# Attention in float32r: two pieces instead of three bfloat16 ones, two heads in the halves of the array's rows, rotation and split on GpSimd

## What is computed

```
qkv = (x @ Wqkv).reshape(b, l, 3, H, DH)          # H = 16 heads, DH = 16
q, k, v = (qkv[:, :, 0], qkv[:, :, 1], qkv[:, :, 2])
q = q * cos + rotate_half(q) * sin
k = k * cos + rotate_half(k) * sin
scores = jnp.einsum('bqhd,bkhd->bhqk', q, k) * DH ** -0.5
attn = jax.nn.softmax(scores, axis=-1)
out = jnp.einsum('bhqk,bkhd->bqhd', attn, v).reshape(b, l, d) @ Wo
x = _layernorm(x + out)
...                                                # RMS norm, shared block, top-2 of 8 experts
x = _layernorm(x + ffn(x))
```

## Time and profile before

| | us |
|---|---|
| median of 3 runs | 1294.05 (1291.84 to 1295.58) |
| span of the profiled execution, first to last instruction | 1291.3 |
| start to first exponential | 53.1 |
| attention, first exponential to the last transposes of its output | 53.1 to 569 |
| everything behind attention | some 722 |

### The profile page before, as it was taken

One profiled execution on the slowest core, in us unless ns is written; L12 is line 12 of the kernel. 1 busy time (PEld: TensorE's weight loads), 2 busy tenths in 40 slices (PEclk: granted clock), 3 DMA queues, 4 the chain that ended last, 5 costly groups with the idle time before them and its releaser, 6 DMA issues. The chain is left out here.

```text
span 1291.3 us, 29542 instructions
## 1 busy us (share of the span) xinstructions
PE 1224.3 (95%) x9440; PEld 934.5 (72%) x9440; DVE 976.6 (76%) x1925; ACT 996.4 (77%) x2043; POOL 583.9 (45%) x590
## 2 busy tenths in 40 slices
PE   4899999999999999979899969999999999999997
PEld 3444444444444444337899969999999999999897
DVE  6888887888788888728676648777777777777596
ACT  6699998999899999846654437777777777777687
POOL 6332322232223220005467745666666666666763
PEclk8899999999999999988899979999999999999999
DMA  9300000010000000433022246777777777776363
GB/s 298 117 19 19 18 19 20 2 35 3 19 2 19 2 18 3 144 104 117 18 91 100 87 158 197 260 251 253 246 238 238 235 249 253 253 239 217 101 218 119
DMA packets 125414, 161.28 MB, mean 125 GB/s; under 512 B 17088, under 2 KB 108224, under 8 KB 125312
## 3 DMA queue, kind: packets, MB, share of 16 engines
q1 hardware_dynamic: 118496, 141.25, 33.7%
q0 software_dynamic: 6816, 18.75, 4.1%
HBM read 122.06 MB, written 37.52 MB: 124 GB/s over the span
## 5 line engine op out<-in xcount | busy, mean ns | idle before, releaser
L546 DVE TENSOR_REDUCE att_mx<-att_psA 128x1 f32<-128x512 f32 x512 | 337.8, 683 | 75.5 <-PE att_psA L331 74.9
L461 ACT ACTIVATE att_prob<-att_psB 128x512 f32<-128x512 f32 x512 | 299.7, 600 | 54.0 <-PE att_psB L341 41.0
L341 PE MATMUL att_psB<-att_qk 128*128 128x512 bf16 x512 | 197.6, 388 | 12.8 <-issue 5.6
L1648 ACT ACTIVATE exp_psU<-exp_psU,ew_b 128x256 f32<-128x256 f32 x312 | 126.6, 447 | 103.7 <-PE exp_psU L1605 103.7
L331 PE MATMUL att_psA<-att_qk 96*128 96x512 bf16 x512 | 196.9, 386 | 3.0 <-DVE att_mx L546 3.0
L1699 DVE CAST exp_hh<-exp_psU 128x512 fp32r<-128x512 f32 x156 | 107.9, 692 | 101.9 <-ACT exp_psU L1648 101.9
L1588 PE MATMUL exp_psD<-exp_w2h,exp_hh 128*128 128x256 f32 x624 | 175.8, 282 | 0.0
L1603 PE MATMUL exp_psU<-exp_xh,exp_w1h 128*128 128x256 f32 x624 | 173.7, 278 | 1.4 <-DVE exp_xl L1690 1.4
L1605 PE MATMUL exp_psU<-exp_xh,exp_w1l 128*128 128x256 f32 x624 | 173.4, 278 | 0.0
L1604 PE MATMUL exp_psU<-exp_xl,exp_w1h 128*128 128x256 f32 x624 | 173.3, 278 | 0.0
L1589 PE MATMUL exp_psD<-exp_w2l,exp_hh 128*128 128x256 f32 x624 | 172.4, 276 | 0.0
(11 more groups left out here) (215 smaller groups left out, 3244.9 us busy)
## 6 DMA issues: line engine op xcount, KB each, us to landing
ew_w<-ew SPq DMA_DIRECT2D x40, 1024.0 KB, 6.1
exp_w<-ew SPq DMA_DIRECT2D x38, 1024.0 KB, 5.8
slots_x<-pre_acc SPq DMA_DIRECT2D x13, 780.0 KB, 10.8
pre_spare<-slots_x SPq DMA_DIRECT2D x39, 260.0 KB, 4.1
out_g<-rows_y SPq DMA_DIRECT2D x32, 256.0 KB, 4.1
ew_b<-eb SPq DMA_DIRECT2D x39, 128.0 KB
pre_spare<-xT SPq DMA_DIRECT2D x8, 512.0 KB, 4.5
attn_rows<-att_ob SPq DMA_DIRECT2D x8, 512.0 KB, 2.8
```

The costliest lines, as they stand in the source:

```text
L341: pe.matmul(psB[B_BANK[n % U]][:, :], r[:, 1, kt * P:(kt + 1) * P], r[:, 0, :], start=True, stop=True).then_inc(s_bmm, 1)
L461: act.activation(prob[:, n % PR, :], psB[B_BANK[n % U]][:, :], ACT.Exp, scale=SCALE).then_inc(s_exp, 1)
L546: dve.reduce_max(mx[:, g % 2, n % U:n % U + 1], psA[A_BANK[n % U]][:, :], AX_X).then_inc(s_max, 1)
```

## The change

The diff below is cut; what is left out is renaming, the prologue's counterparts, and tiles that moved in memory.

```diff
-    TERMS = 6
+    TERMS = 3
     KR = TERMS * DH
+    KM = KR + 2
+    PAIR_COLS = 64 + KR
...
-    QK_LEAD, V_LEAD = 6, 4
+    QK_LEAD, V_LEAD = 7, 4
...
-    T_LEAD = A_LEAD + 5
-    PIECES = 3
-    PROJECT_QK, ROPE, COPY_OUT, TURN_OUT, NORM_OUT = (0, 1), (1, 2, 3), 3, 5, (5, 6)
-    PROJECT_V, COPY_V, SPLIT_MAX, TURN_MAX, COPY_MAX = 13, 13, 8, 10, 9
-    PIECE_1, PIECE_2, SPREAD, SPLIT_X = 6, 10, 0, 12
+    T_LEAD = A_LEAD + 17
+    TURNS = 4
+    PIECES = 2
+    PROJECT_QK, COPY_QK, COPY_OUT, TURN_OUT, NORM_OUT = (0, 1), 2, 3, 5, (5, 6)
+    PROJECT_V, COPY_V, TURN_MAX, SPLIT_MAX = 13, 13, 9, (9, 10)
...
+    COLS_ORDER = (1, 0, 3, 2)
+    ROWS_ORDER = (0, 1, 2, 3)
...
-        stack = a.sb("stack", [P, 2, NT, 2, H, KR], BF16)
-        qk = a.sb("qk", [P, RING, 2, G, L], BF16)
+        stack = a.sb("stack", [P, 2, NT, 2, H // 2, PAIR_COLS], F32R)
+        qk = a.sb("qk", [P, RING, 2, 2, L], F32R)
...
+        def rows_of(g, i, j, n):
+            first = 64 * (j % 2)
+            return qk[first:first + n, g % RING, i, j // 2, :]
...
-                for k in range(PIECES):
-                    sp.dma_start(qk[96 + k:97 + k, g % RING, 0, :, :]...
+                for half in range(2):
+                    for k in range(PIECES):
+                        r = 64 * half + KR + k
+                        sp.dma_start(qk[r:r + 1, g % RING, 0, :, :]...
...
+            def split_x(b, it):
+                ...
+                pass_on(xt[:, b % 2, 0, 0:2])
+                pool.tensor_copy(xh[:, b % 2], xt[:, b % 2]).then_inc(s_xh, 1)
...
                 pool.tensor_tensor(xl[:, b % 2], xt[:, b % 2], xh[:, b % 2].bitcast(F32), ALU.subtract).then_inc(s_xl, 1)
+            def turn_pairs(tile, it):
+                ...
+                pool.tensor_tensor(o[:, :, 0:half], x[:, :, half:], table(sin, 0, half), ALU.mult).then_inc(s_rot, 1)
+                pool.tensor_tensor(o[:, :, half:], x[:, :, 0:half], table(sin, half, DH), ALU.mult).then_inc(s_rot, 1)
+                pool.tensor_tensor(x, x, table(cos, 0, DH), ALU.mult).then_inc(s_rot, 1)
+                pool.tensor_tensor(rr[:, tile % 2, :], xc, rs, ALU.add).then_inc(s_rr, 1)
+            def split_hi(tile, it):      # 1 tiny op and 4 copies of 128x256
+            def split_lo(tile, it):      # 4 subtractions of 128x128
...
-                pe.matmul(psA[A_BANK[n % U]][:, :], r[:, 0, qt * P:(qt + 1) * P], r[:, 1, :], start=True, stop=True).then_inc(s_amm, 1)
+                pe.matmul(psA[A_BANK[n % U]][:, :], rows_of(g, 0, j, KR)[:, qt * P:(qt + 1) * P], rows_of(g, 1, j, KR),
+                          start=True, stop=True).then_inc(s_amm, 1)
...
-                pe.matmul(psB[B_BANK[n % U]][:, :], r[:, 1, kt * P:(kt + 1) * P], r[:, 0, :], start=True, stop=True).then_inc(s_bmm, 1)
+                pe.matmul(psB[B_BANK[n % U]][:, :], rows_of(g, 1, j, KM)[:, kt * P:(kt + 1) * P], rows_of(g, 0, j, KM),
+                          start=True, stop=True).then_inc(s_bmm, 1)
...
-                    m = pe.transpose(psT[0:KR, half, t * P:(t + 1) * P], stack[:, b % 2, t, half, h % H, :], ident[:, :])
+                    m = pe.transpose(psT[0:PAIR_COLS, t * P:(t + 1) * P],
+                                     stack[:, b % 2, t, i, g % HG * 2 + pair, :].bitcast(F32), identf[:, :])
...
-                act.activation(qk[0:KR, g % RING, :, h % G, :], psT[0:KR, :, :], ACT.Copy).then_inc(s_tev, 1)
+                act.activation(qk[0:PAIR_COLS, g % RING, i, pair, :], psT[0:PAIR_COLS, :], ACT.Copy).then_inc(s_tev, 1)
...
+            def copy_qk(tile, it):
+                dve.tensor_copy(xc, psX[:, :]).then_inc(s_qrd, 1)
```

More of the change, by code:

```diff
@@ L202, in heads_of, with halves, of_half, term @@
         def heads_of(t):
[L203 to L207 removed]
+            return t.rearrange("p (h d) -> p h d", d=DH)
+        def halves(b, t, i):
+            blocks = stack[:, b % 2, t, i]
+            return [blocks[:, :, 64 * half:64 * half + KR] for half in range(2)]
+        def of_half(t, i, half):
+            return t[:, i * D:(i + 1) * D].rearrange("p (k h d) -> p k h d", h=2, d=DH)[:, :, half, :]
+        def term(cols, m):
+            return cols[:, :, m * DH:(m + 1) * DH]
+        def hi_terms(cols, i):
+            first, last = (Q_TERMS, K_TERMS)[i][0]
+            return cols.rearrange("p k (m d) -> p k m d", d=DH)[:, :, first:last + 1:last - first, :]
+        def lo_term(cols, i):
+            return term(cols, (Q_TERMS, K_TERMS)[i][1])
+        def twice(t):
+            return t.unsqueeze(2).to_broadcast([P, H // 2, 2, DH])
+        def rows_of(g, i, j, n):
+            first = 64 * (j % 2)
+            return qk[first:first + n, g % RING, i, j // 2, :]
         block = pr.block
@@ new lines, in split_hi @@
+            def split_hi(tile, it):
+                b, t = tile // NT, tile % NT
+                if t == 0:
+                    wait(pool, it, s_tmm, TURNS * HG * (b - 1), TURNS)
+                wait(pool, it, s_rr, tile + 1, 1)
+                pass_on(rr[:, tile % 2, 0:2])
+                for i in range(2):
+                    for half, cols in enumerate(halves(b, t, i)):
+                        pool.tensor_copy(hi_terms(cols, i), twice(of_half(rr[:, tile % 2, :], i, half))).then_inc(s_hi, 1)
@@ L298, in period @@
+            def split_lo(tile, it):
+                b, t = tile // NT, tile % NT
+                for i in range(2):
+                    for half, cols in enumerate(halves(b, t, i)):
+                        wait(pool, it, s_hi, 4 * tile + 2 * i + half + 1, 4)
+                        pool.tensor_tensor(lo_term(cols, i), of_half(rr[:, tile % 2, :], i, half), term(cols, 0).bitcast(F32),
+                                           ALU.subtract).then_inc(s_stk, 1)
             def period(p, it):
@@ L318, in _ @@
-            groups(pool, period)
+                if valid(tile, NT * B):
+                    if tile >= FILL:
+                        turn_pairs(tile, it)
+                        split_hi(tile, it)
+                    split_lo(tile, it)
+                b = (tile + 1) // NT
+                if (tile + 1) % NT == 0 and valid(b - 2, B - 2):
+                    split_x(b, it)
+            groups(pool, period, passes=PASSES - 1)
         @block.tensor
@@ L381, in turn_max @@
                 take_psX(g - 1, MAX, it)
-                wait(pe, it, s_msp, g + 1, 1)
-                pe.matmul(psX[0:PIECES * U, 0:P], mstk[:, :, :].rearrange("p m u -> p (m u)"), ident[:, :], start=True, stop=True).then_inc(s_mtr, 1)
+                wait(pe, it, s_max, U * (g + 1), U)
+                pe.transpose(psX[0:U, 0:P], mx[:, g % 2, :], identf[:, :]).then_inc(s_mtr, 1)
             def add_pv(g, kt, it):
@@ L494, in x_hi @@
-            def x_hi(b, it):
-                v = 16 * (b // 2 + 1)
-                act.wait_ge(s_x[b % 2], v if it is None else v + it * 16)
-                wait(act, it, s_vmm, NT * (b - 1), 1)
+                act.wait_ge(s_rr, tile + 1)
+                for i in range(2):
+                    for half, cols in enumerate(halves(b, t, i)):
+                        act.activation(hi_terms(cols, i), twice(of_half(rr[:, tile % 2, :], i, half)), ACT.Copy).then_inc(s_hi, 1)
+            def x_hi(b):
+                act.wait_ge(s_x[b % 2], 16)
```

274 lines of the change are left out of this document (104 added, 170 removed).

## The result

| | before | after |
|---|---|---|
| median, us | 1294.11 (4 runs, 1291.84 to 1295.58) | 1312.5 (4 runs, 1305.92 to 1324.04) |
| after to before | | 1.0162, 95% interval [1.0100, 1.0224] |
| span of the profiled execution, us | 1291.3 | 1304.0 (own time 1306.09) |
| period of attention, transposition of the maxima to the next | 16.0 | 16.5 |
| first of these transpositions, last one | 47.6, 545.7 | 47.4, 553.8 |

What follows compares the result with a forecast made beforehand. PE was taken as the bound: 16.00 - 6.93 + 3.78 + 1.98 = 14.8 us a period. Thirty periods gave -35, POOL +6, prologue -3: -32 us, so 1262 us, 8-in-10 range 1214 to 1330.

Steps and rivals of the forecast that it cites:

- What bounds it: Attention period: PE is the bound, busy all 16.00 us before and expected busy throughout 14.8 us after.
- The pair: Score matmuls: the two in the two row halves run together, so 16 pairs cost 3.78 us a period.
- 18 switches x 0.11 = 1.98: PE in a period: 18 changes between 64-row and full tiles at 0.11 us each, 1.98 us.
- loads hidden: PE at switches: weight loads stay hidden, so a switch costs only 0.11 us; forecast's own case, chance 0.42.
- 12.85: Attention period: PE's work in us after the change, without the switches.
- Rival 2: PE's short runs: switches also expose weight loads, 17.9 us a period, 1348 us; half hidden 16.4, 1303 us; chance 0.19.
- Transposes even: PE in a period: 8 x 0.23 us of transposes go and 4 x 0.45 come, so no change.
- ACT and DVE: Attention period: ACT needs 10.4 us and DVE 11.4 us, neither late at 14.8 us.
- POOL late, +6: Periods where x is split: PE waits 1.0 us for POOL, six times, +6 us.
- Prologue -3: Before attention: POOL, DVE and ACT lose work on the first tiles, POOL gains rotations; -3 us (ends -8 and +5).
- The end of attention is costed at nothing: Last groups of attention: the same chain of waits as before, costed at 0 us.
- Rival 4: Behind POOL's six waits the clock falls to 1.2 GHz, losing 12 us: 1274 us; chance 0.06.

Runs made afterwards that it cites:

- experiment 1: Changed kernel with both score matmuls of a unit taking the same half of the rows: 1367.53 us (one run).
- Experiment 2: Changed kernel with all score matmuls reading 65 rows from partition 0, in full 128x128 tiles; does not compute attention: 1317.44 us (one run).
- Experiments 9 and 10: SP issues the next stage's loads behind the last placement of the maxima: 9 on the eight-run kernel, 1272.1 us; 10 on the changed kernel, 1313.97 us.
- four-block kernel: Changed kernel with all other PE work of a period gathered in four blocks, leaving runs of four score pairs: 1419.2 us.
- eight-run kernel: Changed kernel with the thirteen blocks of other PE work joined to eight, leaving eight runs of two score pairs: 1276.41 us.

## Why the prediction was wrong

- **What bounds it: right.** PE was busy 16.48 of 16.53 us.
- **The pair: right.** 0.01 us between the two starts, and in experiment 1 a single pair that shares a half costs one matmul of 0.24 more.
- **"18 switches x 0.11 = 1.98": the step that failed.** The forecast took 0.11 a switch with the loads hidden. By PE's timeline the 13 runs pay 2.7 us beyond 0.236 a pair (ten single pairs 0.20 each, three runs of two 0.19 to 0.32), the nine other blocks 1.07 (0.11 to 0.18 each, 0.05 the smallest one), the wait for ACT 0.3, and 0.38 goes off again, because the 0.09 ahead of each V block is now part of the pair before it. That is 3.7 us on top of 12.85, as measured. Experiment 2 gives 3.4 for the changes by another way, and its weight loads show that the assumption "loads hidden" failed. The 0.11 was read from the entry into column strips; no row showed a row tile. Rival 2 had named the mechanism, and its sign came: a single pair takes over 0.4 us from block to block. That its 16.4 us "with half of it hidden" lies so near the 16.53 is partly luck, since the half was a guess and 0.3 us of the period is the wait for ACT. What I held against it, that the V block shows little of it, did not carry over: the V block still takes 0.99 to 1.00, and it is the pair beside it that pays (0.43).
- The Trainium skill, TensorEngine Tiling (Array Packing), section Key Properties, says that a change of the tiling mode drains the engine. The trace agrees that each change costs time, and the runs give it the price that decides here: 0.19 us each with float32r operands.
- **Transposes even: right in themselves** (0.35 to 0.45 for four), as were projections.
- **ACT and DVE: right.** 11.5 and 12.1 us busy a period, forecast 10.4 and 11.4; an exponential is recorded with 0.60, not 0.48. But ACT was not quite in time: behind the maxima, where three pairs follow with one short block between them, PE waits 0.3 us a period for it.
- **POOL late, +6: did not occur.** POOL's rows in the changed kernel, a period in which x is split:

```profile
326.40 0.73 POOL L335 TENSOR_TENSOR pre_acc<-pre_acc,att_sin 128x256 f32<-128x256 f32 x1 [9.06 <-DVE pre_acc L624]
...
330.75 1.43 POOL L351 CAST att_stack<-att_rr 128x256 fp32r<-128x256 f32 x4
...
333.94 1.03 POOL L320 CAST att_xh<-pre_spare 128x1024 fp32r<-128x1024 f32 x1
335.06 2.39 POOL L323 TENSOR_TENSOR att_xl<-pre_spare,att_xh 128x1024 fp32r<-128x1024 f32 x1
```

  A copy of 256 columns costs 0.36 in a row of four (I took 0.5), one of 1024 columns 1.03 (I took 1.6; its low end, 1.0, was right). From POOL's start to its end it is 11.05 us, not 12.2, and the longer period helps: x is split at 337.45, and PE's projection of it starts at 338.8. 1.4 us are left. At 14.8 us a period this would have been late, by about 0.3.
- **Prologue -3:** the first maxima came 0.2 us earlier, no more, and the first exponential 1.9 us later (54.9 for 53.1). What ate the gain was not tried.
- **"The end of attention is costed at nothing": wrong, 8.9 us in the profiled execution.** The earlier trace rows showed the wait; I priced its fourth DMA and not what lies behind a wait. Experiments 9 and 10 put 9.0 and 4.9 us on the loads ahead of it; in the changed kernel 4.0 us are left with the DMA wait gone, at half the clock.
- **Rival 4 had the right mechanism at the wrong place.** POOL made nobody wait. The clock fell at the start of a pass, behind waits of about 1 us for ACT, in one profiled execution and not in the other. The median lies about 6 us above the profiled execution, most likely by such falls; only the mean clocks speak for that, since the slower executions have no trace. Why the kernel before keeps its clock there more often (1291.84 to 1295.58) was not tried.

By the spans, the forecast was 1291.3 - 32 = 1259.3 and 1304.0 came, 44.7 more: the periods +43.3 (8.3 longer instead of 35 shorter; 16.53 us for 14.8 alone would be 30 x 1.73 = 52, of which the starts of the passes give back 4.4 and the last periods, with fewer blocks between, most of the rest), POOL -6, prologue +2.8, the end of attention +8.9, the stages behind it -4.3.

## What to carry to other kernels

Before packing small matmuls in row tiles, count how often the stream changes between tile sizes: a run of packed matmuls has to save more than 0.19 us at each end, so one pair of 512 columns between two full-size blocks does not (with its block of transposes 1.01 us in the changed kernel, 0.92 in the full tiles of experiment 2), and two pairs do (1.24 against 1.36). But a run may be only as long as the PSUM banks and the consumers' latency carry it: beyond that PE waits, and the clock can fall behind the waits. Where a chain of DMAs ends a stage, issue the next stage's bulk loads behind it, not ahead of it.

## What the runs showed of the hardware

- A pair of float32r matmuls of 512 columns in the two 64-row halves starts 0.01 us apart. A pair costs 0.43 us between full-size blocks and 0.33 each in a run of two.
- Entering or leaving a 64-row tile costs 0.19 us on average. Behind the change the weight load (0.19 us long) begins with its matmul and not 0.22 us ahead of it, and the matmul is recorded 0.11 us longer.
- The clock's reply to the same waits differs between executions: 0.94 and 0.54 us of waiting were followed by some 14 us at 0.50, 1.03 and 0.68 us by none.
- In the four-block kernel PE stood idle 12% of a stretch of 400 us, and the clock granted over it was 0.94; in the eight-run kernel it was idle 2% and the clock 0.99.
